# Window attention on Trainium2: both halves of the weighted sums in one run, the transposes after them

## What is computed

```python
h = shift_token(x)
q, k, v = jnp.split(h @ wqkv, 3, axis=-1)      # 8 heads of 64
q = l2norm(q) * qs
k = l2norm(k) * ksc
q, k = rotary_xpos(q, k)
sim = jnp.einsum('bhwid,bhwjd->bhwij', bq, bk) # own window of 128 and the one before
attn = jax.nn.softmax(jnp.where(mask, -big, sim), axis=-1)
o = jnp.einsum('bhwij,bhwjd->bhwid', attn, bv)
x = x + o @ wo
```

## The kernel before

| name | function, line | what PE does | bank | who reads it out |
|---|---|---|---|---|
| X | `transposes` L2241 | next tile's rows turned, 2 transposes | pt | ACT `hidden` L2043 |
| S0 | `scores(turn, 0)` L2273 | scores of heads 0 to 3 | sc | DVE `maxima` L2155, L2160, then ACT `exps` L2063 |
| R | `spread_reciprocals` L2334 | reciprocal denominators of the turn before, 4 transposes | pp[0] | ACT L2079 |
| J | `project` 0 and 1, L2256 | queries and keys of the next tile | pa | DVE `rotate` L2130, L2132, ACT L2048 |
| S1 | `scores(turn, 1)` L2273 | scores of heads 4 to 7, into the banks of S0 | sc | as S0 |
| C0 | `columns(turn, 0)` L2293 | probabilities of heads 0 to 3 turned, 8 transposes | pp | ACT L2069 (even), DVE L2176 (odd) |
| V, O | `project` 2 L2256, `output` L2345 | values of the next tile; output of the turn before | pa, pt | ACT L2056; DVE L2194 |
| C1 | `columns(turn, 1)` L2293 | probabilities of heads 4 to 7 turned | pp | as C0 |
| W0 | `weighted(turn, 0)` L2323 | weighted sums, heads 0 to 3 | po | (after W1) DVE `output` L2187 |
| Q, K | `heads_to_rows` L2303, L2309 | next tile's queries and keys turned, 4 transposes each | pp[0], pp[1] | ACT `queries` L2052, DVE `keys` L2181 |
| W1 | `weighted(turn, 1)` L2323 | weighted sums, heads 4 to 7 | po | as W0 |

## Time and profile before

### The profile page before, as it was taken

How to read it: one execution, slowest core, us unless ns; L and a number is a source line. 1 busy time by engine, 2 the same in 40 slices (tenths; PEclk the granted TensorE clock), 3 DMA queues, 4 the chain that set the end, 5 groups by cost and what they waited for, 6 DMA issues and landing times. The chain is left out here.

```text
span 3995.9 us, 59179 instructions
## 1 busy us (share of the span) xinstructions
PE 3643.4 (91%) x21704; PEld 2593.4 (65%) x21704; DVE 2522.0 (63%) x5386; ACT 1601.5 (40%) x3052; POOL 1392.0 (35%) x1567
## 2 busy tenths in 40 slices
PE   6888878887799999999998998999979989999799
PEld 3666666666455688888886664666645556666465
DVE  4898988899566455555554444777743357777333
ACT  5666666666100122222221213666631146666211
POOL 4778777788100000000000223444411134444111
PEclk8899999999899999999998998999989999999899
DMA  1000000000200100000001112111122011111221
GB/s 39 1 11 12 1 11 11 11 6 6 87 32 32 35 12 12 12 12 12 11 11 55 64 63 64 38 34 37 38 63 64 27 59 33 38 34 34 74 64 37
DMA packets 150197, 129.32 MB, mean 32 GB/s; under 512 B 20804, under 2 KB 147544, under 8 KB 149656
## 3 DMA queue, kind: packets, MB, share of 16 engines
q1 hardware_dynamic: 149912, 125.54, 10.0%
HBM read 87.73 MB, written 37.77 MB: 31 GB/s over the span
## 5 line engine op out<-in xcount | busy, mean ns | idle before, releaser
L830 PEld LDWEIGHTS ssm_pu<-ident,ssm_ub 128*128 128x128 f32 x2048 | 255.8, 150 | 220.3 <-issue 86.0
L830 PE MATMUL ssm_pu<-ident,ssm_ub 128*128 128x128 f32 x2048 | 325.4, 292 | 80.4 <-POOL ssm_ub L322 47.2
L322 POOL TENSOR_SCALAR ssm_ub<-ssm_uT,ssm_bcT 128x512 f32<-128x512 f32 x512 | 356.4, 718 | 96.7 <-ACT ssm_uT L380 63.4
L336 POOL TENSOR_TENSOR ssm_acc<-ssm_acc,ssm_weighted 128x512 f32<-128x512 f32 x256 | 328.4, 1292 | 143.4 <-ACT ssm_weighted L462 143.0
L842 PE MATMUL ssm_pt<-ident,ssm_state 128*128 128x128 f32 x2048 | 288.5, 285 | 82.6 <-DVE ssm_acc L630 58.6
L2256 PE MATMUL win_pa<-win_w_wqkv,win_hT 128*128 128x512 f32 x768 | 357.9, 603 | 1.6 <-ACT win_hT L2043 1.1
L620 DVE TENSOR_TENSOR_SCAN ssm_state<-ssm_da,ssm_carry,ssm_pu 128x512 f32<-128x512 f32 x256 | 312.2, 1260 | 21.2 <-PE ssm_pu L830 16.4
L1838 PE MATMUL glu_up<-glu_hT,glu_w_w 128*128 128x512 f32 x704 | 309.4, 599 | 3.4 <-DVE glu_hT L1761 3.4
L620 DVE TENSOR_TENSOR_SCAN ssm_state<-ssm_da,ssm_pu 128x512 f32<-128x512 f32 x256 | 296.6, 1199 | 25.1 <-PE ssm_pu L830 16.9
L842 PEld LDWEIGHTS ssm_pt<-ident,ssm_state 128*128 128x128 f32 x2048 | 240.4, 147 | 107.9 <-DVE ssm_acc L630 67.8
L2017 POOL TENSOR_TENSOR win_rotated<-win_straight,win_turned 128x512 f32<-128x512 f32 x128 | 163.0, 1274 | 417.0 <-DVE win_turned L2132 417.0
(11 more groups left out here) (241 smaller groups left out, 7295.3 us busy)
## 6 DMA issues: line engine op xcount, KB each, us to landing
win_raw<-in_tables SPq DMA_DIRECT2D x64, 128.0 KB, 2.2
a<-win_y SPq DMA_DIRECT2D x64, 128.0 KB, 1.7
glu_xs<-a SPq DMA_DIRECT2D x32, 256.0 KB, 3.3
glu_x<-a SPq DMA_DIRECT2D x16, 512.0 KB, 5.3
ssm_x<-in_L_attn_x SPq DMA_DIRECT2D x8, 512.0 KB, 3.9
x<-ssm_out SPq DMA_DIRECT2D x16, 256.0 KB, 2.1
moe_x<-x SPq DMA_DIRECT2D x8, 512.0 KB, 3.9
x<-moe_y SPq DMA_DIRECT2D x8, 512.0 KB, 2.9
```

The source lines that it names most:

```text
L322: nc.gpsimd.tensor_scalar(ub[:, i % 2, t, :], uT[:, k % 2, t, :], bcT[:, k % 2, t, n:n + 1], 1.0, ALU.mult, ALU.mult).then_inc(ub_ready.se ...
L336: nc.gpsimd.tensor_tensor(acc[:, k % 2, t, :], acc[:, k % 2, t, :], weighted[:, j, :], ALU.add)\
L830: last = nc.tensor.transpose(pu[c][:, t * P:(t + 1) * P], ub[:, i % 2, t, c * P:(c + 1) * P], ident)
```

## The change

Three moves, and nothing else; no instruction is added, removed or altered. On DVE the copy of C1's odd half goes ahead of the scaling of the next tile's keys. On PE R goes ahead of S0, and W1 goes ahead of Q and K, directly behind W0.

```diff
--- before.py
+++ after.py
@@ -2209,10 +2209,9 @@
                     residual(turn.before())
                 dve.wait_ge(exp_ready.sem, exp_ready.at(turn.i))
                 nc.vector.reciprocal(rden[:, :], den[:, :]).then_inc(rden_ready.sem, 1)
+                columns(turn, 1)
                 if more:
                     unit_keys(turn.next())
-                columns(turn, 1)
-                if more:
                     keys(turn.next())
 
             first = Turn(0, 0)
@@ -2348,9 +2347,9 @@
             def body(turn, before, more, more2):
                 if more:
                     transposes(turn.next())
-                scores(turn, 0)
                 if before:
                     spread_reciprocals(turn.before(), True)
+                scores(turn, 0)
                 if more:
                     project(turn.next(), 0)
                     project(turn.next(), 1)
@@ -2362,9 +2361,9 @@
                     output(turn.before(), turn.next() if more else None)
                 columns(turn, 1)
                 weighted(turn, 0)
+                weighted(turn, 1)
                 if more:
                     heads_to_rows(turn.next(), turn)
-                weighted(turn, 1)
 
             first = Turn(0, 0)
             transposes(first)
```

## The result

The changed kernel takes 4003.52 us (median of 22 runs, 3998.80 to 4005.52) against 3996.91 for the one before (22 runs): ratio 1.0015, 95% interval 1.0009 to 1.0022. Run again beside other kernels it took 4001.33 against 3996.48, ratio 1.0012 (1.0003 to 1.0021). So it is slower by 5 to 7 us, within the 0.2% that I called the same; the forecast was 3999.0, with a range of 3992 to 4008. The profiled execution took 4001.79, its span 3999.9.

What follows compares the result with a forecast made beforehand. PE was taken to set the pace in regular turns, with the S0-to-S1 chain almost binding. Per stage +1.2 (regular), +0.23 (last), -0.43 (first) gave +1.0, for both +2.0: 3999.0 against the median, range 3992 to 4008.

Steps and rivals of the forecast that it cites:

- Q at 2.93, K at 3.43: Regular turn, us from C1's start: Q starts at 2.93 instead of 1.99, and K at 3.43, no longer stalling.
- R at 4.37 by the queries' copy, S0 at 4.93: Regular turn: R waits for ACT's copy of the queries until 4.37; S0 starts at 4.93, 0.23 us later than before.
- S0 to S1 at 4.90, the turn 0.04 longer: Regular turn: maxima and exponentials between S0 and S1 take 4.90 us and set S1; 29 turns add 1.2 per stage.
- First turn -0.43: First turn of a stage: S1 comes at 2475.47 instead of 2475.90, 0.43 us less.
- It takes the whole delay of S0: +0.23: Last turn of a stage: S1 follows S0 by 4.90 before and after, so S0's delay adds 0.23 us.
- a few us either way: Stage borders: allowance for the low clock spell at a stage's end falling otherwise at this and later borders.
- The price of a short spell: Stage's end: the low clock spell costs 1.2 us in S1 and the transposes behind it.
- The first, PE's work as the only limit: Rival, all turns: only PE's own work limits, S1 at 9.39, 0.40 less a turn, 25 us less, 3972; chance 0.03.
- The second, a looser chain: Rival, S0 to S1: chain looser than read, S1 at 9.52, 17 us less, 3980; chance 0.06.
- the third rival: Rival, regular turns: PE's stalls lower the clock, 8 us from one turn in nine, 4017 at every fourth; chance 0.05.
- The fourth, late hand-overs: Rival, mid-turn: the two copies hand over to PE late, near 0.30 us, giving 4009; chance 0.05.

## Why the prediction was right, and where it was off

*Q at 2.93, K at 3.43.* Right: 2.93 and 3.42. The last turn of before had shown the run of 32 with DVE's copy unhindered, and it was the same in every turn.

*R at 4.37 by the queries' copy, S0 at 4.93.* Right: 4.37 and 4.92. It is R, and not the keys, that decides by a little: where R stood behind S0, the keys' copy let S0 start at 4.86, so the 4.93 for the keys was 0.07 too late. The hand-over of 0.14 from ACT to PE, which I had taken between 0.04 and 0.30, measured 0.14 (2605.32 to 2605.46).

*S0 to S1 at 4.90, the turn 0.04 longer.* Right in mechanism and nearly in size: 4.92, and 15.28 against 15.22. The two kernels without row sums show that this chain sets the turn after the change and did not before. PE's own need between S0 and S1 was 4.69 and not 4.59, which made no difference, as the chain needs more.

*First turn -0.43.* Right: 16.12 against 16.55.

*"It takes the whole delay of S0: +0.23"*, the last turn. This is the term that was mis-sized: it measured +1.70 and +1.81. Two things were missing. In the last turn of the kernel before there is no X, so S0 stood at 4.33 after C1 and not at 4.70, while in the changed kernel the copies hold it at 4.93 with or without X: the delay is 0.60. And the clock stayed low for about 7 us instead of 3.5, 1.08 and 1.21 more between S1 and C1; I had allowed for the spell to fall otherwise, "a few us either way", and not for its being longer in both stages. That the change makes it longer is not shown: kernels with R on either side of S0 had both lengths. The price of a short spell was too low as well, 1.2 for two groups where the whole way from S1 to C1 loses 1.6. With both put in, and the regular turns at the measured 0.057 for 0.04, the sum is 5.7 instead of 2.0, and 4002.7 against the median. The measured difference of 4.9 to 6.6 against the 2.0 of the forecast is inside the range, whose upper end was set for late hand-overs; that it also had room for the last turns is luck.

*The rivals.* The first, PE's work as the only limit, is excluded: S1 came at 9.84 and not at 9.39, and the two kernels without row sums show why. It holds in part: with the chain out of the way a turn took 15.07, 0.15 below the kernel before. X between Q and K, where it adds no switch of shape, costs 0.15 less than between W1 and S0. TensorEngine Tiling (Array Packing) of the Trainium skill, section Key Properties, says that a change of tiling drains TensorE; the runs agree in kind. But the change bought fewer such switches with later copies. The second, a looser chain, is excluded by the 4.92 from S0 to S1, where it asked for 4.59. The clock did fall, as in the third rival, but only in the last turns; in the regular ones it stayed at 1.00. The fourth, late hand-overs, did not come.

## What to carry to other kernels

When an engine looks 99% busy and a reordering shortens its work, look for the chain that leaves the engine and comes back: here producers for other engines (Q, K) had been placed early and a consumer's filler (R) in the chain's shadow, and grouping by kind undid both. The edges of a loop, where pieces of the body are missing, show such chains bare in the trace of the kernel before, and they need a sum of their own. A change of several moves should be taken apart: one of these three is worth 20 us, and the other two gave it back and 5 to 7 us more.

## What the runs showed that I had not expected

- An edit after C1 moved work that stands before it: with R ahead of S0, POOL's reciprocal roots for the next tile come 0.2 us earlier relative to C1, which made two of my expected turns 0.1 and 0.2 too long.
- J's eight matmuls take 3.63 to the next group directly behind the scores, and 3.53 behind a run of transposes.
- 3.7 us of discarded matmuls in each of two turns made the changed kernel 4 to 7 us faster (3996.94 against 4001.33 and 4003.52), by keeping the clock at its upper level there.
- A spell at the lower clock lasted 6.8 us where it began at least 0.5 us before S1, and 3.4 us where it began at most 0.17 before S1 or behind it, in all 22 last turns that had one.
